# A new order for the steps of a turn, with some steps moved to another depth of the pipeline

## The reference

```python
x = x + tanh(g_xattn) * xattn(layernorm(x), ctx, ctx)
x = x + tanh(g_ffn)   * ffn(layernorm(x))
```

```python
f_q, f_k, f_v = proj(q), proj(k), proj(v)      # layer norm, then @ w_in.T, 8 heads
mixed = (cw + vw * decorr_scale) * dots / (|f_q| |f_k|) + ww * q_ratio * k_ratio
out = (mixed @ f_v) @ w_out.T + b_out
```

```python
attn = softmax(q k^T / sqrt(256))      # over the second axis of scores laid out (k, q)
z = l2(l2((attn @ v) @ Wo) @ Wff)
out = gelu(z)
```

## Time and profile before

| | us |
|---|---|
| median of 3 runs | 1366.68 |
| lowest, highest | 1365.57, 1370.45 |
| the profiled execution, its time | 1367.6 |
| the profiled execution, its span | 1365.9 |
| TensorE busy | 1210.3 |
| VectorE busy | 1113.9 |
| ScalarE busy | 1008.8 |
| GpSimd busy | 194.1 |

### The profile page before, as it was taken

How to read it: one execution, slowest core, us unless ns; L and a number is a source line. 1 busy time by engine, 2 the same in 40 slices (tenths; PEclk the granted TensorE clock), 3 DMA queues, 4 the chain that set the end, 5 groups by cost and what they waited for, 6 DMA issues and landing times.

```text
span 1365.9 us, 34600 instructions
## 1 busy us (share of the span) xinstructions
PE 1210.3 (89%) x10386; PEld 756.1 (55%) x10386; DVE 1113.9 (82%) x3180; ACT 1008.8 (74%) x3334; POOL 194.1 (14%) x160
## 2 busy tenths in 40 slices
PE   4999877898989999999999898989898989898875
PEld 2667556564646565646465656565555556565531
DVE  6986655797979797979797979898888979797854
ACT  5766232587878696969687878787887878787787
POOL 2352120102020202010110101010102020202000
PEclk9999889999999999999999999999999999999976
DMA  8440032727263625454443536271708071726341
GB/s 254 144 148 19 4 58 70 205 44 210 51 194 67 187 73 171 90 164 96 144 116 120 141 98 162 77 184 55 206 26 218 20 229 27 216 45 175 73 125 47
DMA packets 247888, 162.30 MB, mean 119 GB/s; under 512 B 94538, under 2 KB 235559, under 8 KB 247848
## 3 DMA queue, kind: packets, MB, share of 16 engines
q1 hardware_dynamic: 247848, 161.80, 43.1%
HBM read 86.74 MB, written 42.58 MB: 95 GB/s over the span
## 4 chain that ended last, share of the span: by engine, by line
PE 43%; DVE 24%; issue 13%; ACT 3%; DMA 1%; DVEq 1%; SPq 1%; PEld 0%; ACTq 0%; POOLq 0%; POOL 0%; PEldq 0%
PE work L893 12%; PE work L895 11%; PE work L894 11%; DVE nm L1716 6%; PE attended L1434 5%; DVE md L1670 3%; PE score L1423 3%; ACT prob L1519 2%; DVE mTl L1623 2%; DVE l2s L1685 1%; DVE norm L1610 1%; DVE VTl L1623 1%; PE work L1331 1%; DVE zb L1752 1%; DVE x2S L1679 1%
## 5 line engine op out<-in xcount | busy, mean ns | idle before, releaser
L1519 ACT ACTIVATE prob<-score,nm 128x256 f32<-128x256 f32 x1024 | 477.1, 495 | 58.7 <-DVE nm L1716 57.3
L1716 DVE TENSOR_REDUCE nm<-score 128x2 f32<-128x512 f32 x512 | 336.6, 680 | 20.3 <-PE score L1423 18.6
L1519 ACT ACTIVATION_READ_ACCUMULATOR prob<-score,nm 128x1 f32 x1024 | 233.0, 228 | 0.0
L1636 DVE BATCH_NORM_STATS2 qst<-work 128x6 f32<-128x128 f32 x512 | 112.2, 283 | 92.2 <-PE work L895 92.1
L1434 PE MATMUL attended<-prob,vsp 128*32 128x256 f32 x2048 | 139.9, 399 | 17.6 <-DVE vsp L1731 17.6
L1423 PE MATMUL score<-qstack,kstack 64*128 64x256 f16 x1024 | 102.4, 286 | 17.9 <-ACT prob L1519 13.0
L1574 POOL TENSOR_TENSOR rq<-qft,mhalf 128x32 f32<-128x32 f32 x16 | 86.8, 5427 | 159.7 <-DVEq L1643 159.7
L893 PE MATMUL work<-wTh,xTh 128*128 128x512 f16 x256 | 97.1, 379 | 4.1 <-DVE xTl L1630 3.1
L895 PE MATMUL work<-wTh,xTl 128*128 128x512 f16 x256 | 97.0, 379 | 0.0
L894 PE MATMUL work<-wTl,xTh 128*128 128x512 f16 x256 | 97.0, 379 | 0.0
L1434 PEld LDWEIGHTS attended<-prob,vsp 128*32 128x32 f32 x2048 | 55.6, 112 | 73.0 <-DVE vsp L1731 28.8
(11 more groups left out here) (327 smaller groups left out, 3273.4 us busy)
## 6 DMA issues: line engine op xcount, KB each, us to landing
qstack<-parts SPq DMA_DIRECT2D x64, 256.0 KB, 3.7
kstack<-parts SPq DMA_DIRECT2D x64, 256.0 KB, 4.1
sqE<-sq_rows SPq DMA_DIRECT2D x64, 154.0 KB
s_xin<-in_x SPq DMA_DIRECT2D x8, 1024.0 KB, 6.1
xin<-in_x SPq DMA_DIRECT2D x16, 512.0 KB, 3.6
x2S<-in_x SPq DMA_DIRECT2D x16, 512.0 KB, 3.5
parts<-qh SPq DMA_DIRECT2D x32, 256.0 KB, 2.7
parts<-ql SPq DMA_DIRECT2D x32, 256.0 KB, 2.9
```

Source lines behind the costliest of these rows:

```text
L1519: nc.scalar.activation(prob[:, g % PG, e, j + jj, :], sc[n % SC][:, jj * NQ:(jj + 1) * NQ], ACT.Exp, bias=nm[:, u + jj:u + jj + 1], accum_ ...
L1636: last = nc.vector.bn_stats(qst[:, t, 4 * half + h, :], bank(e)[:, h * DH:(h + 1) * DH])
L1716: nc.vector.tensor_reduce(nm[:, u:u + 2], sc[n % SC][:, :].rearrange("p (u q) -> p u q", q=NQ), AX.X, ALU.max, negate=True).then_inc(max_r ...
```

## The change

The steps of a turn get another order, in all three lists. Twenty-two steps change their depth: G1, G2, G4, G5 with their halves, `qs1`, `qpow` and `rk` go from 1 to 0, `S0`, `S1` and `M0` from 2 to 1, `back1`, `back3`, `pv1.v` and `res` from 1 to 2. What decides whether a step belongs to the first or the second part of the code is no longer its depth but its letter (`late`). Some waits name more banks, since the order in which they are emptied has changed. What a step computes stays as it is. HEAD and TAIL are cut here.

```diff
 ORDER = """
-rk V0 qs1 V1 V0.h ldx V0.l S0 qpow V1.h G0 M0 V2 G0.h V1.l X0 M1 a1 V2.h S1 G0.l a1.h V2.l vt0 X1 G1 M2 G2 M3 G1.h S2 G2.h
-a1.l X2 G1.l G3 qs2 X3 G2.l a0 M4 V3 a0.v M5 G3.h aux R0 X4 ldy G3.l S3 z V3.h G4 G5 X5 P0 V3.l G4.h sqe0 G5.h S4 M6
-V4 M7 X6 G4.l X7 M8 V5 wq G5.l V4.h S5 M9 d0 X8 R1 M10 X9 P1 V4.l V5.h M11 sqe1 S6 X10 fk0 V5.l vt1 M12 X11 M13 fk1 E0
-d0.o X12 R2 S7 d1 fk0.h L0 M14 fk1.h X13 fk0.l P2 fk1.l m0.h M15 X14 S8 d2 m0.l X15 M16 d3 d1.o X16 d2.o d4 M17
-m1.h R3 m2.h X17 m1.l d5 m2.l S9 S10 d3.o P3 d4.o m3.h M18 y0 m4.h m3.l X18 M19 d5.o X19 M20 m4.l m5.h X20 m5.l S11
-M21 zT0 y1 M22 zT0.h R4 E1 zT0.f L1 y0.o X21 M23 X22 zT0.l zT1 y1.o X23 S12 fk2 ln1 zT1.h P4 fk2.h zT1.f O0 M24 lpow
-M25 X24 S13 R5 X25 ln2 P5 O0. S14 fk2.l zz0 zT1.l E2 zz1 zz0.h M26 q0 zz1.h zz0.l X26 zz1.l q1 M27 M28 X27 pk0 q0.o
-q1.o pq0 pk0.h M29 X28 pk0.l S15 X29 pk1 M30 M31 X30 pq1 L2 R6 X31 P6 pq0.h R7 pk1.h pq0.l P7 pq1.h pk1.l parts0 O1 E3
-L3 pq1.l O2 O1. parts1 O3 O2. q2 O3. back0 q3 F1 q2.o pv0 q3.o F2 back3 q4 pv0.v back1 q5 q4.o back2 F3 q6 q5.o q7
-q6.o pv1 q7.o F4 pv1.v out res
+pv1.v res qs2 V2 G3 V2.h a0 X0 V2.l back1 G0 G3.h M1 G3.l a0.v X1 M2 V1 V4 G0.h aux V1.h M3 G0.l V1.l sqe0 X2 S2 M4 M5
+V0 a1 V4.h V4.l X3 V0.h X4 a1.h R0 S3 V5 P0 X5 M6 V0.l V5.h V3 V3.h a1.l M7 sqe1 X6 V5.l S4 M8 d0 M9 d1 V3.l X7 vt0 X8
+d0.o ldy R1 d2 X9 S5 wq d1.o m0.h vt1 M10 M11 m1.h m0.l m1.l X10 P1 X11 S6 E0 fk1 M12 fk1.h M13 X12 d2.o fk1.l d3 d3.o
+S7 d4 M14 m2.h m2.l d5 M15 ldx X13 X14 fk0 S8 L0 R2 P2 m3.h d4.o M16 m3.l M17 X15 m4.h S9 y0 d5.o X16 z M18 X17 fk0.h
+R3 S10 m5.h M19 zT0 fk0.l P3 X18 y0.o m4.l m5.l M20 zT0.h fk2 X19 zT1 zT0.f fk2.h zT0.l E1 fk2.l S11 R4 M21 zT1.h
+back3 y1 zT1.f zT1.l q0 M22 X20 X21 rk M23 y1.o q1 q0.o q2 L1 X22 O0 ln1 X23 S12 R5 q1.o M24 O0. q2.o lpow P4 M25 ln2
+P5 q3 q3.o q4 X24 zz0 S13 X25 q4.o M26 S14 zz0.h zz1 q5 zz1.h zz0.l q6 X26 M27 zz1.l X27 M28 E2 X28 M29 X29 q5.o S15
+M30 q6.o M31 R6 X30 pq0 X31 L2 pq0.h pk0 q7 R7 pk0.h pq0.l pk0.l P6 P7 O1 E3 L3 q7.o O1. O2 O3 qs1 O2. parts0 pk1
+back0 O3. G4 pq1 pk1.h pk1.l F1 G4.h G4.l qpow pq1.h G5 F2 G5.h back2 pq1.l G2 G2.h G5.l G2.l F3 G1 pv0 parts1 S0
+pv0.v M0 F4 S1 pv1 G1.h out G1.l
 """.split()
 
 HEAD = """
-fk0 +rk ldx fk1 fk0.h fk1.h z fk0.l zT0 +ldx fk1.l zT0.h zT1 zT0.f zT1.h fk2 zT0.l zT1.f fk2.h zT1.l q0 q1 q0.o q2
-q1.o fk2.l q3 q2.o q4 q3.o q5 q4.o +z q6 q5.o q7 q6.o q7.o +G0 +G0.h +V0 +qs1 +V1 +V0.h +qpow +V0.l +V1.h +G0.l +V2
...
+fk1 rk fk0 fk1.h fk1.l fk0.h fk0.l ldx fk2 z fk2.h zT0 zT1 fk2.l zT0.h zT0.f zT1.h zT0.l zT1.f zT1.l q0 q0.o q1 q2
+q1.o q3 q2.o q3.o q4 G5 q4.o q5 q5.o +ldx q6 q6.o G4 G4.h G4.l q7 G2 G5.h G5.l G2.h q7.o qs1 G1 G1.h qpow G2.l G1.l
++V2 +G3 +qs2 +V2.h +a0 +V2.l +a0.v +G0 +G3.h +G3.l +G0.h +V4 +V1 +V1.h +G0.l +V4.h +ldy +V1.l +V4.l +V0 +V0.h +a1 +V5
++a1.h +V5.h +V0.l +aux +V3 +sqe0 +a1.l +d0 +V3.h +V3.l +V5.l +d1 +d0.o +sqe1 +fk1 +d2 +d1.o +m0.h +m0.l +d2.o +fk1.h
++vt1 +m1.h +d3 +m1.l +fk1.l +d3.o +vt0 +m2.h +d4 +m3.h +m2.l +fk0 +z +d5 +fk0.h +m3.l +fk0.l +wq +d4.o +d5.o +rk +m4.h
++zT0 +y0 +m4.l +m5.h +m5.l +zT0.h +y0.o +zT0.f +fk2 +fk2.h +zT1 +zT1.h +zT0.l +zT1.f +y1 +fk2.l +zT1.l +y1.o +q0 +q1
++ln1 +q2 +q0.o +q1.o +q2.o +q3 +lpow +ln2 +q3.o +q4 +zz0 +zz0.h +q4.o +zz1 +zz0.l +zz1.h +q5 +zz1.l +q5.o +pq0 +pq0.h
++pk0 +q6 +pq0.l +pk0.h +pk1 +pk0.l +pk1.h +q6.o +q7 +pk1.l +parts0 +G4 +G4.h +G5 +q7.o +G5.h +qs1 +pq1 +back0 +pq1.h
++G4.l +G2 +G5.l +pv0 +G2.h +pq1.l +G1 +G2.l +pv1 +G1.h +qpow +S0 +S1 +parts1 +G1.l +M0 +pv0.v +back2
 """.split()
 TAIL = """
-rk S0 S1 V0 M0 qs1 G0 V0.h V1 X0 V0.l qpow G0.h M1 V1.h V2 M2 X1 V1.l V2.h S2 G0.l X2 a1 V2.l vt0 G1 M3 a1.h G2 G1.h a1.l
-G2.h G1.l X3 G3 qs2 G2.l a0 G3.h M4 S3 a0.v V3 M5 X4 aux G3.l M6 X5 G4 M7 wq X6 S4 R0 G5 M8 P0 X7 M9 sqe0 V3.h R1
...
+V2 back1 back3 qs2 pv1.v M1 X0 V2.h G3 G3.h X1 a0 V2.l res a0.v M2 G0 aux S2 G0.h G3.l V1 M3 X2 sqe0 X3 M4 M5 V1.h
+G0.l V4 V4.h V0 S3 R0 V1.l a1 X4 V0.h M6 V4.l a1.h P0 V5 X5 S4 V5.h sqe1 M7 X6 X7 a1.l d0 V0.l M8 V5.l S5 M9 X8 ldy R1
+X9 P1 M10 S6 M11 X10 d0.o X11 V3 M12 V3.h M13 E0 X12 R2 X13 d1 V3.l S7 M14 L0 P2 M15 S8 m0.h X14 vt0 d1.o m1.h m0.l
+M16 d2 d3 d2.o X15 M17 S9 m1.l d4 m2.h M18 X16 wq M19 d5 X17 m2.l X18 S10 vt1 R3 X19 d3.o d4.o M20 m3.h m4.h m3.l M21
+P3 m4.l E1 X20 X21 S11 d5.o M22 m5.h y0 S12 m5.l M23 M24 X22 y0.o y1 M25 X23 R4 L1 R5 S13 y1.o P4 P5 O0 X24 E2 ln1
+lpow M26 X25 O0. M27 X26 ln2 S14 M28 zz0 X27 M29 zz0.h zz1 zz1.h zz0.l X28 S15 zz1.l L2 pq0 M30 M31 X29 X30 X31 pk0 R6
+pq0.h R7 pq0.l P6 P7 pk0.h E3 pk0.l parts0 L3 O1 O1. O2 O3 back0 back2 O2. O3. pk1 pk1.h pq1 pk1.l F1 S0 pv0 pq1.h F2
+pv1 S1 pq1.l M0 parts1 F3 +M1 pv0.v F4 +X0 +pv1.v +X1 +M2 +M3 +X2 +S2 +back1 +M4 +X3 +S3 +M5 +X4 +X5 +R0 +P0 +M6 +X6
++M7 +S4 +X7 +M8 +S5 +M9 +R1 out +X8 +X9 +P1 +S6 +M10 +M11 +X10 +X11 +E0 +M12 +M13 +L0 +S7 +X12 +X13 +R2 +M14 +P2 +M15
...
+MOVED = {step: n for n, steps in {0: "G1 G1.h G1.l G2 G2.h G2.l G4 G4.h G4.l G5 G5.h G5.l qpow qs1 rk", 1: "M0 S0 S1", 2: "back1 back3 pv1.v res"}.items() for step in steps.split()}
 CHUNKS = [s for s in ORDER if any(t.startswith(s + ".") for t in ORDER)]
 A_INDEX = {name: k for k, name in enumerate(CHUNKS)}
 WORK_USES = [len(range(s, len(CHUNKS), WORK)) for s in range(WORK)]
 
 
+def late(step):
+    return step[0] in "SMXRPELOF" or step == "out"
+
+
 def lead(step):
 
-    if step[0] in "SMXRPELOF" or step == "out":
+    if step in MOVED:
+        return MOVED[step]
+    if late(step):
         return 2
     return 0 if step.split(".")[0].rstrip("0123456789") in ("z", "zT", "fk", "q", "ldx") else 1
 
...
@@ -1088,7 +1091,7 @@
     z_ready = sem("z_ready")
     qsq_ready, rq_ready, wqr_ready, sq_ready = sem("qsq"), sem("rq_ready"), sem("wqr_ready"), sem("sq_ready")
     v2_ready, r2_ready, zz_ready = sem("v2_ready"), sem("r2_ready"), sem("zz_ready")
-    hi_ready = [sem("hi_first"), sem("hi_ready")]
+    hi_ready = [sem("hi_first"), sem("hi_second"), sem("hi_third")]
     parts_stored, x2_in, y_in = [sem("parts_first"), sem("parts_second")], sem("x2_in"), sem("y_in")
     stack_in = [sem(f"stack{g}") for g in range(4)]
     sc_ready, max_ready, exp_done = sem("sc_ready"), sem("max_ready"), sem("exp_done")
@@ -1112,15 +1115,22 @@
     def latest(names):
 
         last = {}
-        for name in sorted(names, key=A_INDEX.get):
+        for name in sorted(names, key=lambda name: (lead(name), A_INDEX[name])):
             last[A_INDEX[name] % WORK] = name
         return last.items()
 
+    def none_before(pair):
+        return isinstance(pair, int) and pair < 0
+
     def wait_filled(eng, pair, *names):
+        if none_before(pair):
+            return
         for s, name in latest(names):
             eng.wait_ge(filled[s], uses(name, pair) + 1)
 
     def wait_drained(eng, pair, *names):
+        if none_before(pair):
+            return
         for s, name in latest(names):
             eng.wait_ge(drained[s], uses(name, pair) + 1)
 
@@ -1135,6 +1145,12 @@
 
     def key_cols(half, lo_h, hi_h):
         return fk[half][:, lo_h * PM:hi_h * PM].rearrange("p (n c) -> p n c", c=MK)
+
+    def halved(e, pair):
+
+        n = lead(e + ".h")
+        done = halves(running["order"], n)
+        return hi_ready[n], pair * len(done) + done.index(e) + 1
 
     def emptied(e, half):
 
@@ -1167,7 +1183,7 @@
     def run(eng, a_part, b_part, passed=None):
 
         def part_of(s, pair):
-            (b_part if lead(s) == 2 else a_part)(s, pair)
+            (b_part if late(s) else a_part)(s, pair)
 
         def short_turns(first, order):
             running["order"] = order
@@ -1360,7 +1380,8 @@
                 elif kind == "d":
                     b2, tiles = c // 3, HM_TILES[c % 3]
                     if c == 0:
-                        wait_drained(pe, a, "G5")
+                        wait_drained(pe, a, *(f"G{n}" for n in range(6)))
+                        pe.wait_ge(xT_ready, a * KT + KT)
                     for n, t in enumerate(tiles):
                         r = HM_ROWS[t]
                         for k in range(KT):
@@ -1385,13 +1406,13 @@
                                             Vp, (slice(0, Y_ROWS[t]), c, t), t == 0, t == HT - 1)
                 elif kind in ("pq", "pk"):
                     if e == first_projection(running["order"]):
-                        wait_drained(pe, a, "zz1")
+                        wait_drained(pe, a, "zz0", "zz1")
                     for k in range(KT):
                         last = products(nc, bk[:, :], w["w" + kind[1]], (ALL, k, slice(c * P, (c + 1) * P)), zzT, (ALL, k),
                                         k == 0, k == KT - 1)
                 elif kind == "pv":
                     if e == first_projection(running["order"]):
-                        wait_drained(pe, a, "zz1")
+                        wait_drained(pe, a, "zz0", "zz1")
                     for r in range(2):
                         for k in range(KT):
                             last = products(nc, bk[:, r * DIM:(r + 1) * DIM],
```

(17 more changed lines are left out.)

21 lines of the change are left out of this document (3 added, 18 removed).

## The result

The changed kernel takes 1384.0 us in the median of six executions, the kernel before 1368.0 beside it; 1357.5 was forecast. Without one of the six, which took 2017.0 us at a granted clock of 0.56, its median is 1381.6 and the ratio of the means 1.0109, 95% interval 1.0087 to 1.0131: 1.1% slower.

What follows compares the result with a forecast made beforehand. VectorE was taken to bound the long part of a turn, TensorE the end part. Turns of 70.7 instead of 70.94 (-3.4 us over 14) plus HEAD and TAIL cut the span by 9, giving 1357.5 us; range 1328 to 1380.

Steps and rivals of the forecast that it cites:

- sqE, Vp and xin each land 1 to 4 us before use: Long part of the turn: these loads arrive 1 to 4 us early, so no engine waits for them.
- rival 2: Loop: VectorE packs the long part as before, 0.4 us idle; turn 68.5 to 70, time 1327 to 1348; chance 0.27.
- the end part: Turn from the end of M31, 17.95 us: VectorE's idle time falls from 7.3 to 5.35 us, 1.9 won.
- the long one: Rest of the turn, 52.75 us: VectorE works 50.6 and idles 2.15 where it idled 0.4, 1.75 lost.
- the prices start to start: Step costs counted between starts of neighbouring instructions; VectorE's steps come to 63.2 us a turn, 7.7 idle.
- HEAD: Code ahead of the loop: q0 starts 3.2 us later, other waits shrink; S1 ends near 252.5, G1.l at 253.4.
- d0.o stays at about 210: HEAD: d0.o keeps its start because a chain through sqE sets it, though q0 starts 3.2 us later.
- TAIL: Code behind the loop: 46.4 us to M31, X0 at 1304.3, then 52.6 to the span's end at 1356.9.
- The table load: Loop start: ScalarE's load costs 1.28 us ahead of pv1.v, without the drain of about 1.38 the Trainium skill gives.
- 4: Loop: the score chain starves because S12 comes late on TensorE; at +2.5 us a turn, 1392 us; chance 0.17.
- 5: Loop start: switching the table costs more than its row, 1.28 us a turn, giving 1375 us; chance 0.03.
- 3: Whole kernel: no gain, turn 70.9, the ends' gains eaten by HEAD's late z; 1360 to 1373; chance 0.13.

Runs made afterwards that it cites:

- a_nosqe: Changed kernel without the twelve loads of sqE and SyncE's wait for the store; the multiply of d takes a constant: 1330.9 us.
- a_sqelast: Changed kernel with the twelve loads of sqE issued last in SyncE's queue, unread; the multiply of d takes a constant: 1336.8 us.
- a_nowait_ldx: Changed kernel with a constant in d's multiply, so no wait for sqE, and the load of xin moved right behind aux: 1363.3 us.
- a_pv1end: Changed kernel with pv1.v moved from the start of the turn to its end, ahead of the table load: turn 71.68 us.
- a_reslate: Changed kernel with res, a copy of 512 KB, issued behind sqe1 instead of ahead of the store of sqT: not faster, time not given.
- c_pool: Changed kernel, computing everything, with seven of the twelve loads of sqE issued by GpSimd instead of SyncE: turn 2.0 us longer.
- b_nosqe: Kernel before the change without the twelve loads of sqE; the multiply of d takes a constant: 1362.9 us.

## Why the prediction was wrong

**The step that failed** is one sentence: "sqE, Vp and xin each land 1 to 4 us before use". It was put down without a layout of SyncE's queue. Beside it, the list of what moves named rk, qpow, pv1.v, res, back1 and back3, but not that ldx and vt0 went from ahead of the store of aux, ldy from right behind it and wq from between sqe0 and sqe1, all to behind sqe1. No rival covered it either. By a_nosqe the line costs 2.85 us a turn (71.68 against 68.83), where it cost 0.05 before: 37 us in thirteen turns. By a_sqelast it goes with the loads' place in the queue and not with the bytes alone. The cost shows at three steps in turn, and taking one away only passes it on: d0.o and d1.o (sqE), then z (xin), then y0 (Vp and mT), which still waits 1.0 us in a turn of a_nowait_ldx and not at all in a_nosqe. How the 2.85 divide between the store's landing, the issues and the slower transposes stays open.

**The rest of the turn was better than forecast.** I forecast 70.7; without the line it is 68.83, in rival 2's band of 68.5 to 70. That the turn missed by only 1.0 (71.68) is two errors of opposite sign: 2.85 for the line, 1.87 the other way. Summed over one turn of a_nosqe, the gaps of over 0.12 us between neighbouring instructions of VectorE come to 6.9, where I had 7.5: 4.5 in the end part (5.35 forecast), 2.4 in the long one (2.15). VectorE's own work is then 62.0, where the prices start to start gave 63.2. So two thirds of the surplus, by this count, are work put too high. Part of it is a slip in the prediction's first paragraph: the turn whose rows it read runs from 609.58 to 680.08, 70.50 us, and its idle time of 7.7 was taken from the average of 70.94. The same count of gaps in that turn gives 62.5 of work. The mechanism, q out of the end part, was right: `qst` no longer waits, S0 is released by TensorE's own queue, and M0 waits 1.75.

**HEAD** failed by 12.2 us at the first F1 (315.1 forecast). "d0.o stays at about 210": it starts at 214.1, since the store of aux goes out at 204.2 and not at 200.2. It does gain 1.9 by no longer standing behind the transposes, but `rq` starts 5.9 later (196.5 against 190.6). The traces divide that into 2.0 by which q0 starts later, 1.7 for the first products of q at half the clock (eight lie 0.43 apart and not 0.21; the granted clock is 0.50 from 180 to 182, behind 3.46 us without work on TensorE, where the kernel before had 1.28 and a clock of 1.00), and 2.3 for the banks that q4 and q5, and q6 and q7, share (the second of each pair is emptied 2.46 behind the first, where the kernel before has 1.30). No run tests these three apart; moving z or the G brought the store no earlier. The larger part of the 12.2 is the line again, 9.9 of it by a_nosqe. (Against the kernel before, whose HEAD loses 4.5 to its own line, the 10.9 are 5.4 of line and 5.5 of the rest of the order.) I can place 8.3 of the 9.9: y0 at 226.5 in place of 223.4 in a_nosqe (3.1), its products at half the clock (1.7), and the waits of the next turn's d0.o and d1.o (1.59 and 1.94). TensorE's timeline in HEAD shows the clock of y0; products of 256 columns lie 0.21 apart from 227.4 to 230.8, after TensorE's waits for the d of 1.8, 1.7 and 2.1 us, and 0.11 before and after:

```profile
228.84 0.42 PE L893 MATMUL work<-Vph,mTh 128*128 128x256 f16 x1
229.06 0.42 PE L894 MATMUL work<-Vpl,mTh 128*128 128x256 f16 x1
```

0.21 for 256 columns is the lower of the two levels, 1.2 GHz; the granted clock from 227.4 to 230.9 is 0.51.

**TAIL** came out near: 120.7 us from the last turn's F1, 122.7 forecast, 126.8 before. Some of this is luck too. The line costs TAIL 3.5 (a_nosqe has 117.2), which nobody forecast, and the rest of it was 5.5 better than laid out.

**The table load** stands in the new kernel's rows as the prediction read it in the old: it starts at 693.79 and pv1.v at 695.09, 1.30 later. That G3 goes late behind it costs nothing that shows: a_pv1end took it out of pv1.v's way and the turn stayed at 71.68. But with VectorE held for sqE, and V2's high half still behind the load, this is a weak test.

Of the rivals, 2 has the turn without the line in its band, but by luck: its reason was 0.4 of idle time in the long part, and there are 2.4, as forecast. 4 did not occur (the exponentials wait 10.5 us for VectorE in four turns, 15.1 before), and nothing shows 5; 3 named HEAD's late z, which is the 2.0 by which q0 starts later, of HEAD's 10.9.

## What to carry to other kernels

When an order of steps is rewritten, write out the DMA queue like an engine: each issue with its length, what it waits for, and the deadline of what it brings. A wait inside that queue (here the landing of a small store) delays all that stands behind it, so see what can stand ahead of the waiting entry or in its gap, and whether a long row of dependent loads can stand last. Here that is shown as a cost only (a_nosqe, a_sqelast): none of the orders tried that computes everything got it back.

A wait taken away in an experiment that moves little is not yet innocent: look for the next consumer of the same queue. Taking the whole line away, in both kernels, measured in one pair what the partial edits had not. And before a gain of 2 us is put down to an edit, look at kernels in which that stage is the same.

When one list fixes both the order and the banks, a second order (here HEAD's) takes its banks from the first: check that steps which follow each other there don't share one.

## What the runs showed of the hardware

The issue of a DMA transpose is not a fixed price: in the turns shown 1.41 and 1.51 us in a_sqelast, where no loads of sqE stand ahead of it, 2.13 and 2.96 right behind twelve, 3.35 and 3.50 with a copy of 512 KB between, 2.31 and 4.13 with seven of the twelve issued by GpSimd at the same time. All that stands behind it waits that much longer.

A store of 16 KB with a load that waits for it: the load goes out 1.66 us behind the store in a_reslate, 1.93 in the kernel before, 2.98 in the changed one. In the changed kernel and in a_reslate loads of qstack and kstack stand right ahead of the store; the copy of 512 KB, 2.6 us ahead, is in the changed kernel alone.

GpSimd issued seven such loads in 3.67 us; SyncE takes 4.86 for twelve. The loads of sqE in c_pool land 6.0 us after their issue in the median, 4.3 to 13.6.

Without the twelve loads in the middle of the line every turn of the changed kernel takes 68.82 to 68.85 us; with them turns lie between 71.05 and 72.54. Scatter alone is no sign of these loads, though: the old order scatters with and without them (70.50 to 71.39 before, 70.42 to 71.25 in b_nosqe), and what sets it there is not shown.
